# Transformer block on one core: placing feed-forward operands so that the moving operand less the weights is 224 bytes modulo 256

## The chip, the cores and the metric

The kernel runs on one core of a Trainium2 chip. The metric is the device time of one execution in microseconds. Three runs of the kernel before took 2417.2 us in the median, from 2412.65 to 2418.02.

## What is computed

A conditioned transformer block in float32 over 64 sequences of 128 rows, width 512, 16 heads, feed-forward width 2048. The core of the reference:

```python
emb = jax.nn.silu(_sin_emb(timestep)) @ W_ada + b_ada
scale, shift = jnp.split(emb[:, None, :], 2, axis=-1)
x = _ln(src) * (1.0 + scale) + shift
q, k, v = heads of (x @ Wq + bq), (x @ Wk + bk), (x @ Wv + bv)
scores = q k^T / sqrt(HEAD_DIM) + attention_bias, -inf where src_mask
ctx = softmax(scores) @ v
x = x + (ctx @ Wo + bo)
h = _ln(x) * g2 + beta2
ff = _gelu2(h @ W1 + b1) @ W2 + b2          # _gelu2(z) = z * sigmoid(1.702 z)
return x + ff
```

## The kernel before, in words

Five engines run hand-ordered streams of instructions with semaphores between them. No scheduler decides an order. The program has a setup, an attention stage that handles one sequence per half step and writes its result to DRAM, and a feed-forward part in two stages: **up** (h @ W1 and the gate, its results stored to DRAM as `gated`) and **down** (the gate's results @ W2, added to the residual). Both feed-forward stages go over 16 groups of four sequences, with eight units in a group.

Every float32 product is made of three float32r matmuls, high by high, high by low and low by high, of operands that were split beforehand into a high and a low part. In the feed-forward part a 2 x 2 block product is written with seven factor products in place of eight (the Strassen-Winograd scheme). So a unit in either stage has 7 products x 2 halves x 3 = 42 matmuls, each with 128 rows, 128 weight columns and 256 moving columns. `three` issues them and `product` (up) and `down` call it:

```python
1597  def three(out_ap, stat, moving, start, stop):
1598      (sh, sl), (mh, ml) = stat, moving
1599      pe.matmul(out_ap, sh, mh, start=start, stop=False)
1600      pe.matmul(out_ap, sh, ml, start=False, stop=False)
1601      return pe.matmul(out_ap, sl, mh, start=False, stop=stop)
...
1606          last = three(psU[i][:, 0:H], [wc[:, weights.AT[j], h, a, e * P:(e + 1) * P] for h in range(2)],
1607                       [T[u][:, h, b, e, :] for h in range(2)], e == 0, e == 1)
...
          last = three(acc[i][:, half * H:(half + 1) * H], [gs[j % 2][:, h, a, half * P:(half + 1) * P] for h in range(2)],
                       [wc[:, weights.AT[j], h, b, :] for h in range(2)], j == 0 and half == 0, j == J - 1 and half == 1)
```

Going up the factors of the weight matrix, `wc`, are the matmul's weights (the stationary operand), and the factors of the rows, `T0` or `T1` by group, are the moving operand. Coming down, the factors of the gate's results, `gs0` or `gs1` by unit, are the weights, and `wc` is the moving operand. The core loads the weights of the next matmul while the present one streams.

Each of these tensors lies at one address in every partition. All slices that a matmul takes of them begin at a multiple of 256 bytes from the tensor's start (512 bytes for 128 float32 columns, 1024 for 256). So for a given product the difference of the two addresses modulo 256, here called the **residue**, is the same for all its matmuls, for a matmul's own weights and for those of the next.

In the up stage a group of transposes (L246) of the next group's rows stands ahead of two of the eight units, eight transposes each time. Around the matmuls, VectorE and ScalarE empty the accumulators into `gu` and apply the gate, GpSimd adds up parts of `gu`, and SyncE stores a `gu` slot per unit. In the down stage SyncE loads `gated` three units ahead into `gbuf` and slots of `gu`, GpSimd forms two sums, ScalarE rounds to the high part and VectorE takes the low part into `gs` (L1556).

Addresses come from `layer`: tensors are given out one behind another, and `at_once` gives out several and takes them back at once, so that the next call begins at the same place (tensors of different stages share memory). A tensor named `ahead_...`, `over_...`, `end_...` or `zone` is never read or written; it only holds a place.

Of the kernel before, what the change touches and what calls it, by code (L numbers as in the profile page):

```python
# [20 lines left out]
F32 = mybir.dt.float32  # L21
F32R = mybir.dt.float32r
# [5 lines left out]
P = 128  # L28
# [142 lines left out]
def slots(t):  # L171

    return t[:, 0:4, :], t[:, 4:8, :]
# [1485 lines left out]
def layer(nc, d, out):  # L1659

    B, S, DM = d["x"].shape
    CH, H = DM // P, d["bias"].shape[1]
    assert S == P and DM == 4 * P and H == 16 and B % 4 == 0
    resid = nc.dram_tensor("resid", [B, S, DM], F32, kind="Internal").ap()
    ada_rows = nc.dram_tensor("ada_rows", [B, 2 * DM], F32, kind="Internal").ap()
    gated = nc.dram_tensor("gated", [B // 4, 8, P, 10 * P], F32, kind="Internal").ap()
    with ExitStack() as hold, nc.Block() as block, ExitStack() as whole:
        shared = lambda name, shape, dt=F32: whole.enter_context(nc.sbuf_tensor(name, shape, dt))
        ident = shared("ident", [P, P])

        def at_once(*tensors):

            with ExitStack() as used:
                return [used.enter_context(nc.sbuf_tensor(name, shape, dt)) for name, shape, dt in tensors]

        eight = lambda name: (name, [P, 8, 2 * P], F32)
        T1, = at_once(("T1", [P, 2, 7, 2, 2 * P], F32R))
        raw_b, raw_c, raw_d = at_once(*(eight(f"raw1_{n}") for n in "bcd"))
        _, raw_a = at_once(("over_raws", [P, 24, 2 * P], F32), ("raw1_a", [P, 4, 2 * P], F32))
        _, _, r0 = at_once(eight("over_wo_hi"), eight("over_wo_lo"), ("r0", [P, 4, DM], F32))  # L1680
        gs1, gbuf1, u2d, u3d, e5 = at_once(("gs1", [P, 2, 7, 2 * P], F32R), eight("gbuf1"),
                                           *((f"part_{n}", [P, 2, 2 * P], F32) for n in ("u2", "u3", "p5")))
        wo = [shared(f"wo_{part}", [P, CH, DM], F32R) for part in ("hi", "lo")]
        raw_o = shared("raw_o", [P, CH, DM])
        shared("end_T1", [P, 1024])

        turn = [whole.enter_context(nc.psum_tensor(f"turn{i}", [P, CH, P], F32)) for i in range(2)]

        w = at_once(*((f"w{n}_{part}", [P, CH, DM], F32R) for n in "qkv" for part in ("hi", "lo")))
        w = [w[0:2], w[2:4], w[4:6], wo]  # L1690
        r, T0, hTf, b2_bc, p1c, p5c = at_once(("r", [P, 4, DM], F32), ("T0", [P, 2, 7, 2, 2 * P], F32R), eight("hTf"),
                                              ("b2_bc", [P, DM], F32), ("p1c", [P, 2 * P], F32), ("p5c", [P, 2 * P], F32))
        raw2_0, raw2_1, gs0, gbuf0, c1, e2, e4 = at_once(
            eight("raw2_0"), eight("raw2_1"), ("gs0", [P, 2, 7, 2 * P], F32R), eight("gbuf0"),
            *((f"part_{n}", [P, 2, 2 * P], F32) for n in ("c1", "p2", "p4")))
        _, gbuf_x = at_once(("over_gbuf0", [P, 9728], F32), eight("gbuf_x"))
        rd = at_once(*((f"rd{i}", [P, 4, DM], F32) for i in range(2)))
        shared("zone", [P, 12288])
        second = SecondNorm(nc, whole, hold, resid, ident, turn, 4, d["W1"].shape[1], r0, r, hTf, [T0, T1])
        _, wc, gu, s1p = at_once(("ahead_wc", [P, 8], F32), ("wc", [P, 8, 2, 7, 2 * P], F32R), ("gu", [P, 4, 4, 2 * P], F32), ("s1p", [P, 2, 2 * P], F32))  # L1700
        halves = gu[:, :, :, :].rearrange("p (s t) q n -> p s (t q) n", s=2)
        places = (gu, s1p, (p1c, p5c), rd, [gs0, gs1], [gbuf0, halves[:, 1, :, :], halves[:, 0, :, :], gbuf1], gbuf_x,
                  [t[:, :, :] for t in (c1, e2, e4, u2d, u3d, e5)], b2_bc)
        with ExitStack() as ctx:
            sb = lambda name, shape, dt=F32: ctx.enter_context(nc.sbuf_tensor(name, shape, dt))
            bq_s, bk_c, bv_bc = sb("bq_s", [P, CH]), sb("bk_c", [P, CH]), sb("bv_bc", [P, DM])

            wo_in = hold.enter_context(nc.semaphore("wo_in"))
            psD = [ctx.enter_context(nc.psum_tensor("psD0", [P, DM], F32)), turn[1][:, :, :].rearrange("p c k -> p (c k)")]
            first = FirstNorm(nc, ctx, hold, d["x"], ident, turn[0])  # L1710
            xin, adab = (t.rearrange("p (s n) -> p s n", s=8) for t in (
                first.xin[:, :, :, :].rearrange("p u b n -> p (u b n)"), first.adab[:, :, :].rearrange("p b n -> p (b n)")))
            second.turned_early = [xin, adab]
            raws = [(raw_a[:, :, :], first.xn[:, :, :].rearrange("p b (s n) -> p (b s) n", n=2 * P))]
            raws += [slots(t) for t in (raw_d, xin, adab, raw_b, raw_c, raw2_0, raw2_1)]
            weights = Weights(nc, hold, d, raws, wc, 8)
            setup_part(nc, block, hold, d, w, first, ada_rows, bq_s, bk_c, bv_bc, raw_o, wo_in)
            attention_part(nc, block, hold, d, w, first, ada_rows, resid, psD, bq_s, bk_c, bv_bc, raw_o, wo_in, second, weights)

        feed_part(nc, block, hold, d, second, weights, places, resid, gated, turn, out)  # L1720
# [25 lines left out]
```

## Time and profile before

| | before |
|---|---|
| median of 3 runs | 2417.2 us |
| the profiled execution | 2417.7 us |
| its span | 2415.9 us |
| TensorE busy | 2330.2 us (96%), 21,034 matmuls |
| VectorE busy | 1709.8 us (71%) |
| ScalarE busy | 1326.4 us (55%) |
| GpSimd busy | 1880.0 us (78%) |
| mean granted TensorE clock | 0.99 |

The attention stage ends at about 1070 us, the up stage at about 1778 us, and the down stage takes the rest. A matmul's duration in the profile runs from its start to the modelled end of its results, and matmuls overlap; the pace of TensorE is the step from one start to the next, which the timeline's start times give.

### The profile page before, as it was taken

Reading aid. Unit: us, or ns where it says so; the run is one execution under the profiler, and the core shown is the slowest. Engines: PE = TensorE matmul, PEld = TensorE weight load, DVE = VectorE, ACT = ScalarE, POOL = GpSimd, SP = SyncE. Lnnn points to the kernel's source line nnn. Section 1 sums busy time; section 2 is a strip of 40 time slices with the busy share of each in tenths; the row PEclk is TensorE's granted clock in tenths of the full one; section 3 lists DMA queues with packets and bytes.
Section 4 is the critical chain, followed back from the end, with each engine's and each line's share of the span. In section 5 each row is a group of like instructions: output and inputs, shape, how many; then the busy total and the mean of one; then the engine's idle time right before and its main releaser. Section 6 shows DMA issues by size and latency. Waiting matters only on the chain.

```text
span 2415.9 us, 61264 instructions
## 1 busy us (share of the span) xinstructions
PE 2330.2 (96%) x21034; PEld 2193.0 (91%) x21034; DVE 1709.8 (71%) x2864; ACT 1326.4 (55%) x3663; POOL 1880.0 (78%) x1787
## 2 busy tenths in 40 slices
PE   5999999999999999987999999999989999999998
PEld 3888888888888888877999999999979999999998
DVE  5777777777777777767667676767566776666676
ACT  2666666666666666675555555555544443433443
POOL 3777777777777777779777877777898878888886
PEclk9999999999999999998999999999999999999999
DMA  7344444444444444423343434344365656556564
GB/s 239 112 138 142 142 127 126 135 142 142 129 130 138 142 133 126 122 89 124 137 163 148 154 148 159 142 159 154 138 226 174 204 176 202 189 189 205 188 197 131
DMA packets 289442, 372.13 MB, mean 154 GB/s; under 512 B 29072, under 2 KB 203280, under 8 KB 289232
## 3 DMA queue, kind: packets, MB, share of 16 engines
q1 hardware_dynamic: 289232, 369.44, 46.6%
q8 instruction: 118, 1.93, 0.3%
q14 instruction: 92, 0.75, 0.1%
HBM read 251.68 MB, written 117.70 MB: 153 GB/s over the span
## 4 chain that ended last, share of the span: by engine, by line
PE 89%; POOL 3%; DVE 3%; issue 2%; ACT 1%; DMA 1%; SPq 0%; DVEq 0%; POOLq 0%; ACTq 0%
PE up L1600 13%; PE up L1599 13%; PE up L1601 13%; PE psD L956 5%; PE turn L956 5%; PE turn L958 5%; PE turn L957 5%; PE psD L958 5%; PE psD L957 5%; PE psS L985 4%; PE psS L971 3%; PE psC L995 3%; PE turn L1599 2%; PE turn L1600 2%; PE turn L1601 2%
## 5 line engine op out<-in xcount | busy, mean ns | idle before, releaser
L1599 PE MATMUL up<-T,wc 128*128 128x256 f32 x1792 | 507.5, 283 | 14.5 <-DVE gu L1473 7.7
L1600 PE MATMUL up<-T,wc 128*128 128x256 f32 x1792 | 503.6, 281 | 0.0
L1601 PE MATMUL up<-T,wc 128*128 128x256 f32 x1792 | 502.8, 281 | 0.0
L628 POOL TENSOR_TENSOR s<-s,rinv 128x512 f32<-128x512 f32 x254 | 265.1, 1044 | 229.0 <-DVE rinv L823 228.8
L744 ACT ACTIVATE s<-s,nmx 128x128 f32<-128x128 f32 x1024 | 397.4, 395 | 7.3 <-issue 4.3
L1599 PE MATMUL up<-wc,gs 128*128 128x256 f32 x1280 | 354.5, 277 | 2.4 <-DVE gs L1556 2.4
L1599 PEld LDWEIGHTS up<-T,wc 128*128 128x128 f32 x1792 | 339.0, 189 | 18.3 <-DVE gu L1473 8.9
L1600 PE MATMUL up<-wc,gs 128*128 128x256 f32 x1280 | 354.2, 277 | 0.0
L1601 PE MATMUL up<-wc,gs 128*128 128x256 f32 x1280 | 354.0, 277 | 0.0
L688 POOL TENSOR_TENSOR bias<-bias,mneg 128x512 f32<-128x512 f32 x256 | 335.3, 1332 | 11.2 <-DVE mneg L828 11.2
L1600 PEld LDWEIGHTS up<-T,wc 128*128 128x128 f32 x1792 | 339.2, 189 | 0.0
L1601 PEld LDWEIGHTS up<-T,wc 128*128 128x128 f32 x1792 | 338.3, 189 | 0.0
L1556 DVE TENSOR_TENSOR gs<-gbuf,gs 128x768 fp32r<-128x768 f32 (+1 forms) x128 | 177.0, 1407 | 110.8 <-ACT gs L1432 110.8
L1556 DVE TENSOR_TENSOR gs<-gu,gs 128x768 fp32r<-128x768 f32 x126 | 187.7, 1517 | 79.7 <-ACT gs L1432 79.7
L1599 PEld LDWEIGHTS up<-wc,gs 128*128 128x128 f32 x1280 | 241.3, 189 | 2.8 <-DVE gs L1556 2.8
L1600 PEld LDWEIGHTS up<-wc,gs 128*128 128x128 f32 x1280 | 241.3, 189 | 0.0
L1601 PEld LDWEIGHTS up<-wc,gs 128*128 128x128 f32 x1280 | 241.2, 188 | 0.0
L1432 ACT ACTIVATE gs<-gbuf 128x768 fp32r<-128x768 f32 (+1 forms) x128 | 115.5, 948 | 185.2 <-PE up L1601 175.4
L1432 ACT ACTIVATE gs<-gu 128x768 fp32r<-128x768 f32 x126 | 113.9, 950 | 173.1 <-PE up L1601 163.2
L744 ACT ACTIVATION_READ_ACCUMULATOR s<-s,nmx 128x1 f32 x1024 | 199.3, 195 | 0.0
L1279 POOL TENSOR_TENSOR gu<-gu,p5c 128x256 f32<-128x256 f32 x128 | 102.6, 801 | 119.7 <-ACT p5c L1373 82.1
L812 DVE TENSOR_TENSOR s<-psS,bias 128x512 f32<-128x512 f32 x256 | 168.3, 678 | 22.0 <-PE psS L971 20.8
(221 smaller groups left out, 7016.5 us busy)
## 6 DMA issues: line engine op xcount, KB each, us to landing
bias<-in_bias SPq DMA_DIRECT2D x128, 512.0 KB, 5.3
gated<-gu SPq DMA_DIRECT2D x128, 512.0 KB, 2.6
adab<-ada_rows SPq DMA_DIRECT2D x64, 512.0 KB, 5.4
gbuf<-gated SPq DMA_DIRECT2D x64, 512.0 KB, 4.0
gu<-gated SPq DMA_DIRECT2D x63, 512.0 KB, 3.8
xin<-in_x SPq DMA_DIRECT2D x32, 512.0 KB, 5.0
resid<-rout SPq DMA_DIRECT2D x64, 256.0 KB, 2.0
r<-resid SPq DMA_DIRECT2D x16, 1024.0 KB, 6.1
```

Source lines behind the costliest of these rows:

```text
L628: eng.tensor_tensor(s[:, b, heads, :], s[:, b, heads, :], rinv[:, b, heads].unsqueeze(2).to_broadcast([P, HG, S]), ALU.mult).then_inc(done, 1)
L688: pool.tensor_tensor(bias[:, b, heads, :], bias[:, b, heads, :], mneg[:, b, :].unsqueeze(1).to_broadcast([P, HG, S]), ALU.add).then_inc(bi ...
L744: last = act.activation(s[:, b, h, :], s[:, b, h, :], ACT.Exp, bias=nmx[:, b, h:h + 1], accum_out=sums[:, b, h:h + 1])
L812: dve.tensor_tensor(s[:, b, heads, :], psS[g][:, :, :], bias[:, b, heads, :], ALU.add).then_inc(score_ready, 1)
L956: pe.matmul(out, sh, mh, start=start, stop=False)
L957: pe.matmul(out, sh, ml, start=False, stop=False)
L958: return pe.matmul(out, sl, mh, start=False, stop=stop)
L1432: act.activation(gs[s % 2][:, 0, ops, :], t[:, ops.start + 1:ops.stop + 1, :], ACT.Copy).then_inc(s_hi, 1)
L1556: dve.tensor_tensor(gs[s % 2][:, 1, ops, :], t[:, ops.start + 1:ops.stop + 1, :], gs[s % 2][:, 0, ops, :].bitcast(F32), ALU.subtract).then ...
L1599: pe.matmul(out_ap, sh, mh, start=start, stop=False)
L1600: pe.matmul(out_ap, sh, ml, start=False, stop=False)
L1601: return pe.matmul(out_ap, sl, mh, start=False, stop=stop)
```

## The change

Two unused tiles of 48 float32 (192 bytes) are put ahead of `T1` and of `T0`, the unused tile ahead of `wc` grows from 8 to 16 float32 (32 to 64 bytes), and the two place holders `end_T1` and `zone` grow by 256 bytes, so that what lies behind them moves too.

```diff
-        T1, = at_once(("T1", [P, 2, 7, 2, 2 * P], F32R))
+        _, T1 = at_once(("ahead_T1", [P, 48], F32), ("T1", [P, 2, 7, 2, 2 * P], F32R))
...
-        shared("end_T1", [P, 1024])
+        shared("end_T1", [P, 1088])
...
-        r, T0, hTf, b2_bc, p1c, p5c = at_once(("r", [P, 4, DM], F32), ("T0", [P, 2, 7, 2, 2 * P], F32R), eight("hTf"),
+        r, _, T0, hTf, b2_bc, p1c, p5c = at_once(("r", [P, 4, DM], F32), ("ahead_T0", [P, 48], F32), ("T0", [P, 2, 7, 2, 2 * P], F32R), eight("hTf"),
...
-        shared("zone", [P, 12288])
+        shared("zone", [P, 12352])
...
-        _, wc, gu, s1p = at_once(("ahead_wc", [P, 8], F32), ("wc", [P, 8, 2, 7, 2 * P], F32R), ("gu", [P, 4, 4, 2 * P], F32), ("s1p", [P, 2, 2 * P], F32))
+        _, wc, gu, s1p = at_once(("ahead_wc", [P, 16], F32), ("wc", [P, 8, 2, 7, 2 * P], F32R), ("gu", [P, 4, 4, 2 * P], F32), ("s1p", [P, 2, 2 * P], F32))
```

The instructions and their order are the same on every engine. The addresses in a partition, and the residues that follow from them:

| tensor | before | after | moved by |
|---|---|---|---|
| T1 | 17024 | 17216 | 192 |
| T0 | 53888 | 54336 | 448 |
| gs1 | 17024 | 17024 | 0 |
| gs0 | 62080 | 62336 | 256 |
| wc | 95296 | 95840 | 544 |
| gu | 209984 | 210528 | 544 |
| wq, wk, wv | 45696, 62080, 78464 | each + 256 | 256 |
| xT0, xT1 (high) | 134464, 142656 | each + 512 | 512 |

| product | moving less weights, modulo 256, before | after |
|---|---|---|
| up: T less wc | 64 | 224 |
| down: wc less gs | 192 | 224 |
| K and Q projection: xT less wk or wq | 192 | 192 |
| V projection: wv less xT (512 columns) | 64 | 64 |
| output projection: wo less cT (512 columns) | 192 | 192 |

## Rows read from the trace of the kernel before

**Rows 1.** The page: busy time of engines, and the chain that ended last

```profile
PE 2330.2 (96%) x21034; PEld 2193.0 (91%) x21034; DVE 1709.8 (71%) x2864; ACT 1326.4 (55%) x3663; POOL 1880.0 (78%) x1787
...
PE 89%; POOL 3%; DVE 3%; issue 2%; ACT 1%; DMA 1%; SPq 0%; DVEq 0%; POOLq 0%; ACTq 0%
```

**Rows 2.** Stretches: us, busy PE (x instructions), PEld, DVE, ACT, POOL, clock, DMA

```profile
1130.00:1745.00 615.00, 610.37 (x5169) 609.42 (x5168) 411.50 (x863) 343.20 (x649) 482.24 (x607) 1.00 0.40 151
...
1860.00:2416.00 556.00, 546.14 (x4819) 545.94 (x4818) 378.27 (x307) 218.92 (x257) 456.24 (x342) 0.99 0.58 186
```

**Rows 3.** Groups by line: TensorE, L1599 (L1600 and L1601 alike)

```profile
L1599 PE MATMUL up<-T,wc 128*128 128x256 f32 x1792 | 507.5, 283 | 14.5 <-DVE gu L1473 7.7 <-ACT p1c L1368 4.4 <-DVE wc L330 1.3
...
L1599 PE MATMUL up<-wc,gs 128*128 128x256 f32 x1280 | 354.5, 277 | 2.4 <-DVE gs L1556 2.4
...
L1599 PE MATMUL turn<-wc,gs 128*128 128x256 f32 x512 | 142.4, 278 | 10.3 <-DVE gs L1556 5.3 <-DVE wc L330 5.0
```

**Rows 4.** Timeline of TensorE (start us, us, what): up, 180 steps apart

```profile
1504.97 0.28 PE L1599 MATMUL up<-T,wc 128*128 128x256 f32 x1
...
1526.17 0.28 PE L1599 MATMUL up<-T,wc 128*128 128x256 f32 x1
```

**Rows 5.** Timeline: down, first and last, 177 steps apart

```profile
2079.91 0.28 PE L1599 MATMUL up<-wc,gs 128*128 128x256 f32 x1
...
2099.97 0.28 PE L1599 MATMUL up<-wc,gs 128*128 128x256 f32 x1
```

**Rows 6.** Timeline: up, last group, 8 steps apart

```profile
1757.30 0.28 PE L1601 MATMUL up<-T,wc 128*128 128x256 f32 x1
...
1758.21 0.28 PE L1600 MATMUL up<-T,wc 128*128 128x256 f32 x1
```

**Rows 7.** Timeline: down, first group, 37 steps apart

```profile
1784.61 0.28 PE L1600 MATMUL turn<-wc,gs 128*128 128x256 f32 x1
...
1788.97 0.28 PE L1601 MATMUL up<-wc,gs 128*128 128x256 f32 x1
```

**Rows 8.** Timeline: K projection, 6 steps and 10 steps apart

```profile
833.39 0.28 PE L958 MATMUL turn<-xT_hi,wk_lo 128*128 128x256 f32 x1
...
834.07 0.28 PE L958 MATMUL turn<-xT_hi,wk_lo 128*128 128x256 f32 x1
...
835.18 0.28 PE L957 MATMUL psD<-xT_lo,wk_hi 128*128 128x256 f32 x1
...
836.36 0.28 PE L958 MATMUL psD<-xT_hi,wk_lo 128*128 128x256 f32 x1
```

**Rows 9.** Timeline: down, behind a wait, clock at 1.2 GHz, 10 steps apart

```profile
1828.96 0.42 PE L1599 MATMUL turn<-wc,gs 128*128 128x256 f32 x1
...
1831.09 0.41 PE L1600 MATMUL up<-wc,gs 128*128 128x256 f32 x1
```

**Rows 10.** Chain in order of time, up stage: eight transposes

```profile
1404.47 0.87 PE turn L246 x8
```

**Rows 11.** DMA issues: KB each, median us to landing

```profile
gated<-gu SPq DMA_DIRECT2D x128, 512.0 KB, 2.6
...
gu<-gated SPq DMA_DIRECT2D x63, 512.0 KB, 3.8
```

**Rows 12.** Columns as in rows 2: middle of up and down

```profile
1260.00:1680.00 420.00, 420.00 (x3579) 420.00 (x3579) 283.25 (x600) 236.80 (x451) 329.10 (x418) 1.00 0.40 153
1920.00:2340.00 420.00, 420.00 (x3708) 420.00 (x3707) 283.99 (x232) 169.67 (x199) 351.53 (x265) 1.00 0.60 193
```

**Rows 13.** Timeline: V projection, 10 steps, and output projection, 9 steps

```profile
363.03 0.39 PE L957 MATMUL turn<-wv_lo,xT_hi 128*128 128x512 f32 x1
...
365.33 0.39 PE L958 MATMUL turn<-wv_hi,xT_lo 128*128 128x512 f32 x1
...
829.63 0.40 PE L958 MATMUL psD<-wo_hi,cT_lo 128*128 128x512 f32 x1
...
831.73 0.39 PE L958 MATMUL psD<-wo_hi,cT_lo 128*128 128x512 f32 x1
```

## The prediction

> **What bounds the kernel now.** I read the page's busy shares and its chain first, then the busy time by stage, then the start times of single matmuls. TensorE is busy 96% of the span and holds 89% of the chain that ended last [rows 1]. By stage [rows 2], the middle of the up stage has TensorE busy 610 of 615 us and the middle of the down stage 546 of 556 us; every other engine has slack there. So in both feed-forward stages the time is a count of matmuls times the step from one start to the next. (The duration column is no such step: a matmul of 0.28 us starts 0.12 us after the last one, since they are pipelined.)
>
> The two products are made of the same instruction, a float32r matmul of 128 rows, 128 weight columns and 256 moving columns, 5,376 times in each stage: three lines of 1,792 going up, three of 1,280 plus 512 coming down [rows 3]. Their steps differ. Going up, 180 steps of one unbroken stretch take 1526.17 − 1504.97 = 21.20 us, **117.8 ns** each [rows 4]. Coming down, 177 steps take 2099.97 − 2079.91 = 20.06 us, **113.3 ns** each [rows 5]. A slower and a quicker step, 4.45 ns apart: that difference, times the count, is what this change can move.
>
> Is the excess bound to the residue? The residue (moving address less weight address, modulo 256) is 64 going up and 192 coming down. But both steps occur at both. Going up, one short stretch after a wait runs at 0.91 us for 8 steps, 114 ns [rows 6]. Coming down, one stretch runs at 4.36 us for 37 steps, 117.8 ns [rows 7]. The projections of K and Q, also 256 columns and with residue 192, show 10 steps in 1.18 us and, 2 us earlier, 6 steps in 0.68 us [rows 8]. So the residue does not fix the step by itself. The stream of weights for the next matmul and the moving stream of the present one settle into one of two patterns, a stretch keeps the pattern it has fallen into, and the residue at most tilts which. At the clock's lower level the down product takes 2.13 us for 10 steps, 213 ns [rows 9], which is 256 columns at 1.2 GHz with no excess; at the upper level 256 columns alone are 106.7 ns. The excess belongs to the upper clock level and to two streams that meet there, not to the instruction.
>
> **The change part by part.** It removes no instruction, adds none and changes no order on any engine. Only addresses move: T0, T1, wc and what lies behind them.
>
> *Up product.* Its residue goes from 64 to 224. No row shows a 256-column matmul at 224. The nearest rows are those at 192, 32 bytes away, against 96 bytes round the circle from 64; and 192 in its longest stretch is the 113.3 ns step. I take 113.3 ns. Steps that count: 5,169 matmuls between 1130 and 1745 us [rows 2], less about 15 groups of 16 transposes, leaves some 4,930. At 4.45 ns each that is **−21.9 us**. I count nothing for the first and last group (1070 to 1130, 1745 to 1778 us): there TensorE waits for factors and weights that come at their own pace, and a quicker step only lengthens the wait. The bounds of this term: no gain at one end. At the other the lowest step of any full weight load in the trace, the transposes, 8 in 0.87 us, 109 ns [rows 10]: 4,930 × 8.8 = 43 us.
>
> *Down product.* From 192 to 224. By the same nearness it stays at 113.3 ns: 0. Bounds: 109 ns, 4,819 [rows 2] × 4.3 = −20.7 us; 117.8 ns, 4,819 × 4.45 = +21.4 us.
>
> *Everything else that moves.* The attention's tiles move by 256 or 512 bytes, so the residues of its products keep their values: 0. The tiles gu and s1p move by 544 and now start 32 bytes past a multiple of 64. The store of a gu slot lands in 2.6 us and the load of one in 3.8 us [rows 11], while a load is issued three units ahead, 3 × 42 × 113 ns = 14 us; twice the time would still be hidden, and what would show it failing is DVE's idle time ahead of gs. If the up stage shortens by 3.7%, POOL, busy 329 of 420 us there, and DVE, 283 of 420 [rows 12], still have room; the next thing to be late would be POOL's sums in gu, which only lie on the chain in the last group today.
>
> Sum: 2417.7 us (the profiled execution: a span of 2415.9 and 1.8 around it) − 21.9 = 2395.8; that execution lies 0.5 us over the median of 2417.2. Forecast **2396 us**.
>
> **Rivals.**
>
> *Both products get quicker still.* If 224 lets the two streams miss each other altogether, the step is bounded by the weight load alone, 109 ns [rows 10], in both stages: −43 − 20.7, or 2354 us. For it: the change sets both products to one value, and the two known steps look like one and two equal delays over 109 ns (4.3 and 8.8), so none is a natural third pattern. Against it: not one 256-column step near 109 ns stands in the stretches read, at 64 or 192. (The Trainium skill, "TensorE: Matmul & The Clock Gate", section "Wait — 56ns, not 53.3ns?", gives a start-to-start time of N ÷ 2.4 GHz plus about 2.5 ns, which for 256 columns would be an estimate of 109.2 ns; no 256-column row here shows it.)
>
> *Nothing changes.* The pattern is chosen by how a stretch begins, not by the residue. Each up group begins twice behind eight transposes and then falls into the slow step; the down stage begins its long stretch once, at 1831 us [rows 9], and keeps the quick one to the end. If 224 leaves that as it is, the time is 2417 us. For it: one residue shows both steps [rows 6 to 8]. Against it: 256-column stretches at 64 are almost all slow and the down stage's mostly quick. The 512-column projections speak neither way cleanly: V at residue 64 takes 2.30 us for 10 steps, the output projection at 192 takes 2.10 us for 9 [rows 13], 230 against 233 ns, so there 64 is the better one. (The Trainium skill, "TensorE: Matmul & The Clock Gate", section "Step-by-step: what each phase is for", says that TensorE reads moving operand and weights through two independent ports, so that loading the next weights takes nothing from the running matmul. By that rule addresses cannot matter and this rival holds; the trace disagrees at least in this, that one instruction has two steps.)
>
> *Slower: the down product falls into the slow pattern.* Its 5,000-odd matmuls from 1831 us on are one stretch that starts once and never restarts, so one unlucky start at the new residue prices all of them: + 4,819 × 4.45 = 21.4 us with the up product as it is, 2439 us. It decides at the first few steps after 1831 us. For it: the slow step is stable in this very product [rows 7]; and at 512 columns 192 is the worse residue, so nearness may point the wrong way. Against it: that slow stretch lasted only until the next wait, and the long one, begun at the same residue behind a wait at 1.2 GHz [rows 9], ended quick.
>
> *Worse than any pattern seen,* a third delay of the same size in both products: 22 + 43 us more, 2482 us. Nothing in the trace shows it; only the missing rows at 224 leave it open.
>
> **How the numbers follow.** Up quick and down as now, 2396: 0.36. Both at the pace of the weight load, or one of them, 2354 or a little over: 0.20. Nothing changes, 2417: 0.24. Down slow, 2439: 0.15. Worse: 0.05. I leave out the last two, 0.20, and take the range from the second rival's 2354 less the uncertainty of its counts, 2346, to the unchanged time with its spread and a small loss, 2424. Within 0.2% (4.8 us, about what a measurement of this kernel can tell from no change) lies only the rival of no change: same 0.24. Faster 0.36 + 0.20 = 0.56, slower 0.15 + 0.05 = 0.20. With cases of both signs, the likeliest one's own range is 2391 to 2400.
>
> **What would show it.** Right: in the profile after, 180 steps of an unbroken up stretch take 20.4 us in place of 21.20 and 177 of the down stretch still 20.06; up's mean duration falls from 283 and 281 ns to the 277 of the down rows; all else, the attention stage above all, keeps its times. Wrong: up at 117.8 (no change), down at 117.8 (the loss), either at 109 (the larger gain), or a shorter step with new idle time ahead of it from POOL or DVE, which would mean that the up stage has another bound.

## The result, and the profile after

| | before | after |
|---|---|---|
| median | 2415.59 us (4 runs, 2412.65 to 2418.02) | 2444.22 us (4 runs, 2443.21 to 2445.42) |
| profiled execution, and its span | 2417.7 us, 2415.9 | 2443.21 us, 2441.4 |

The ratio after to before is 1.0109, 95% interval 1.0085 to 1.0134: slower, where 2396 us was forecast, and outside the range of 2346 to 2424. The experiments below add something on the time of before: it has two values, about 2417 and about 2438 us, and the four runs of this table all had the lower one.

The page after, busy time of the engines and the chain, laid out as in [rows 1]. TensorE's busy time grew by 29.0 us, the span by 25.5:

```profile
PE 2359.2 (97%) x21034; PEld 2222.6 (91%) x21034; DVE 1741.1 (71%) x2864; ACT 1324.3 (54%) x3663; POOL 1833.6 (75%) x1787
...
PE 90%; POOL 3%; DVE 3%; issue 1%; DMA 1%; ACT 1%; SPq 0%; DVEq 0%; POOLq 0%; ACTq 0%
```

The stretches after, columns as in [rows 2]. First the setup and attention, where TensorE was busy 1032.07 us before, then the middle of up and of down:

```profile
0.00:1070.00 1070.00, 1032.60 (x9970) 903.59 (x9970) 800.46 (x1553) 679.42 (x2626) 792.65 (x698) 0.99 0.45 138
1130.00:1745.00 615.00, 610.47 (x5157) 609.59 (x5156) 406.08 (x862) 343.27 (x650) 478.18 (x605) 1.00 0.40 151
1860.00:2442.00 582.00, 571.65 (x4831) 571.44 (x4830) 410.40 (x307) 220.13 (x258) 412.74 (x343) 0.99 0.56 178
```

Attention is unchanged. In the same 615 us of up, 12 fewer matmuls are done than before, at the same busy time and granted clock. Down does 4,831 of them in 571.65 us of busy time, where before 4,819 took 546.14: each is dearer. The groups by line, beside [rows 3], say the same: up's mean duration went from 283 to 285 ns, down's from 277 and 278 to 282 and 283.

```profile
L1599 PE MATMUL up<-T,wc 128*128 128x256 f32 x1792 | 511.3, 285 | 14.6 <-DVE gu L1473 8.2 <-ACT p1c L1368 3.9 <-DVE wc L330 1.3
...
L1599 PE MATMUL up<-wc,gs 128*128 128x256 f32 x1280 | 360.4, 282 | 2.3 <-DVE gs L1556 2.3
...
L1599 PE MATMUL turn<-wc,gs 128*128 128x256 f32 x512 | 145.1, 283 | 9.8 <-DVE gs L1556 5.0 <-DVE wc L330 4.8
```

The step itself, as in [rows 4, 5], from the timeline after. Up, 171 steps in 1524.96 − 1504.73 = 20.23 us, 118.3 ns:

```profile
1504.73 0.28 PE L1599 MATMUL up<-T,wc 128*128 128x256 f32 x1
...
1524.96 0.28 PE L1599 MATMUL up<-T,wc 128*128 128x256 f32 x1
```

Down, 168 steps in 19.88 us, 118.3 ns:

```profile
2080.04 0.28 PE L1599 MATMUL up<-wc,gs 128*128 128x256 f32 x1
...
2099.92 0.28 PE L1599 MATMUL up<-wc,gs 128*128 128x256 f32 x1
```

At the new residue both products have one and the same step, and it is neither of the two seen before. Step by step it repeats every eight matmuls, alike in both products: 120, 117, 122, 118, 117, 121, 116, 116 ns, mean 118.3.

Summed over all steps between 105 and 127 ns (the pace of TensorE at its upper clock level; start to start, from the trace):

| | step before | step after | steps | gives | stage (first matmul to next stage or end) |
|---|---|---|---|---|---|
| up | 117.75 ns | 118.31 ns | 5,209 | +2.9 us | 689.5 to 693.3 us, +3.8 |
| down | 113.39 ns | 118.33 ns | 5,332 | +26.3 us | 637.4 to 662.6 us, +25.2 |

The two stages grew by 29.0 us, and up began 3.4 us earlier: that makes 25.6 us, where the spans differ by 25.5. Nearly all of the loss is the down product's step.

### The profile page after: what moved, and what is told of

Its sections match the earlier page's. It is cut to its first block, busy times and chain, and to the rows that moved or that the text cites. A ratio compares the mean times of both kernels' runs of the same rounds, so it can differ in the third digit from the quotient of the medians.

```text
span 2441.4 us, 61264 instructions
## 1 busy us (share of the span) xinstructions
PE 2359.2 (97%) x21034; PEld 2222.6 (91%) x21034; DVE 1741.1 (71%) x2864; ACT 1324.3 (54%) x3663; POOL 1833.6 (75%) x1787
## 4 chain that ended last, share of the span: by engine, by line
PE 90%; POOL 3%; DVE 3%; issue 1%; DMA 1%; ACT 1%; SPq 0%; DVEq 0%; POOLq 0%; ACTq 0%
PE up L1599 14%; PE up L1600 14%; PE up L1601 14%; PE psD L956 5%; PE turn L956 5%; PE psD L958 5%; PE psD L957 5%; PE turn L958 5%; PE turn L957 5%; PE psS L985 4%; PE psS L971 3%; PE psC L995 3%; PE turn L1599 2%; PE turn L1601 2%; PE turn L1600 2%; PE turn L136 2%
## 5 line engine op out<-in xcount | busy, mean ns | idle before, releaser
L1599 PE MATMUL up<-T,wc 128*128 128x256 f32 x1792 | 511.3, 285 | 14.6 <-DVE gu L1473 8.2
L1600 PE MATMUL up<-T,wc 128*128 128x256 f32 x1792 | 506.6, 283 | 0.0
L1601 PE MATMUL up<-T,wc 128*128 128x256 f32 x1792 | 506.2, 283 | 0.0
L1599 PE MATMUL up<-wc,gs 128*128 128x256 f32 x1280 | 360.4, 282 | 2.3 <-DVE gs L1556 2.3
L1600 PE MATMUL up<-wc,gs 128*128 128x256 f32 x1280 | 360.1, 281 | 0.0
L1601 PE MATMUL up<-wc,gs 128*128 128x256 f32 x1280 | 360.0, 281 | 0.0
L1599 PEld LDWEIGHTS up<-T,wc 128*128 128x128 f32 x1792 | 340.9, 190 | 17.9 <-DVE gu L1473 9.4
L1600 PEld LDWEIGHTS up<-T,wc 128*128 128x128 f32 x1792 | 341.1, 190 | 0.0
L1601 PEld LDWEIGHTS up<-T,wc 128*128 128x128 f32 x1792 | 341.0, 190 | 0.0
L1556 DVE TENSOR_TENSOR gs<-gbuf,gs 128x768 fp32r<-128x768 f32 (+1 forms) x128 | 198.7, 1578 | 98.1 <-ACT gs L1432 98.1
L1556 DVE TENSOR_TENSOR gs<-gu,gs 128x768 fp32r<-128x768 f32 x126 | 199.3, 1615 | 83.9 <-ACT gs L1432 83.9
L1599 PEld LDWEIGHTS up<-wc,gs 128*128 128x128 f32 x1280 | 241.9, 189 | 2.7 <-DVE gs L1556 2.7
L1600 PEld LDWEIGHTS up<-wc,gs 128*128 128x128 f32 x1280 | 241.8, 189 | 0.0
L1601 PEld LDWEIGHTS up<-wc,gs 128*128 128x128 f32 x1280 | 241.7, 189 | 0.0
L1432 ACT ACTIVATE gs<-gbuf 128x768 fp32r<-128x768 f32 (+1 forms) x128 | 115.3, 946 | 197.7 <-PE up L1601 188.2
```

The lines of the kernel that those rows point to most:

```text
L1432: act.activation(gs[s % 2][:, 0, ops, :], t[:, ops.start + 1:ops.stop + 1, :], ACT.Copy).then_inc(s_hi, 1)
L1556: dve.tensor_tensor(gs[s % 2][:, 1, ops, :], t[:, ops.start + 1:ops.stop + 1, :], gs[s % 2][:, 0, ops, :].bitcast(F32), ALU.subtract).then ...
```

## The experiments

The question was what sets the step. A stretch, below, is a run of matmuls of one product without a wait in it; a long one has 40 steps or more. **Theory** (A in the expectations): the residue, whose values have steps of their own. **Rivals:** the pattern is chosen by how a stretch begins and the residue only tilts it; the product or the absolute addresses decide; or something else that the change moved (gu, s1p) costs the time. All kernels but the last differ from before only in unused places, with the place holders behind them grown as in the change (`end_T1` 1088, `zone` 12352); the pad of T0 is always that of T1, so only T1's line is shown. "Step" is the mean defined above, up / down. A kernel without a number of runs ran once.

**1. The up half as forecast: 192 in both** (T up by 128 bytes).

```diff
-        T1, = at_once(("T1", [P, 2, 7, 2, 2 * P], F32R))
+        _, T1 = at_once(("ahead_T1", [P, 32], F32), ("T1", [P, 2, 7, 2, 2 * P], F32R))
```

> Residue 192 in both products, nothing else changed. If the residue alone sets the step (theory A): up and down both step at 113.3 ns, time 2417 - 5,220 x 4.4 ns = about 2394 us. If the product, by the way its stretches begin, sets the step at 64 and 192 (rival B): up stays at 117.8, down at 113.3, about 2417 us. If any common residue for both products hurts (rival C, the change's loss comes from T and gs or wc sharing a bank in some other way): slower than 2430 us.

2411.86 us, before beside it 2410.6. Step 116.18 / 113.49. Up is a mixture at this residue: of its long stretches, 15 run at 113.3 to 113.9 and 22 at 117.8 ns. In the timeline of this kernel, 171 steps of a slow one in 20.14 us, then 159 of a quick one in 18.02 us:

```profile
1499.79 0.28 PE L1599 MATMUL up<-T,wc 128*128 128x256 f32 x1
...
1519.93 0.28 PE L1599 MATMUL up<-T,wc 128*128 128x256 f32 x1
...
1539.93 0.28 PE L1599 MATMUL up<-T,wc 128*128 128x256 f32 x1
...
1557.95 0.28 PE L1599 MATMUL up<-T,wc 128*128 128x256 f32 x1
```

So 192 gives the up product the quick step, but not always.

**2. The residues exchanged: 192 going up, 64 coming down** (wc up by 128 bytes).

```diff
-        _, wc, gu, s1p = at_once(("ahead_wc", [P, 8], F32), ("wc", [P, 8, 2, 7, 2 * P], F32R), ("gu", [P, 4, 4, 2 * P], F32), ("s1p", [P, 2, 2 * P], F32))
+        _, wc, gu, s1p = at_once(("ahead_wc", [P, 40], F32), ("wc", [P, 8, 2, 7, 2 * P], F32R), ("gu", [P, 4, 4, 2 * P], F32), ("s1p", [P, 2, 2 * P], F32))
```

> The residues of the kernel before exchanged: 192 going up, 64 coming down. Theory A: the steps exchange too, up 113.3 and down 117.8 ns, time within 3 us of the kernel before. Rival B: up keeps 117.8 and down 113.3 ns, the same time. The profile's steps tell them apart, not the time.

2436.38 us, before beside it 2410.6. Step 117.33 / 117.78. The down product at 64 has taken over the up product's step, 171 steps in 20.14 us:

```profile
2079.78 0.28 PE L1599 MATMUL up<-wc,gs 128*128 128x256 f32 x1
...
2099.92 0.28 PE L1599 MATMUL up<-wc,gs 128*128 128x256 f32 x1
```

That rules out the product as the cause of before's two steps: 64 is 117.8 ns in either. Up at 192 is again a mixture, here mostly slow. The time missed the forecast, which had the two steps merely exchanged.

**3 to 5. Other residues alike in both products.** 128 and 0 by wc alone (its pad 56 or 24 float32 in place of 8), 160 by T1's pad of 16 and wc's pad taken away:

```diff
+        _, wc, gu, s1p = at_once(("ahead_wc", [P, 56], F32), ("wc", [P, 8, 2, 7, 2 * P], F32R), ("gu", [P, 4, 4, 2 * P], F32), ("s1p", [P, 2, 2 * P], F32))
...
+        _, wc, gu, s1p = at_once(("ahead_wc", [P, 24], F32), ("wc", [P, 8, 2, 7, 2 * P], F32R), ("gu", [P, 4, 4, 2 * P], F32), ("s1p", [P, 2, 2 * P], F32))
...
+        _, T1 = at_once(("ahead_T1", [P, 16], F32), ("T1", [P, 2, 7, 2, 2 * P], F32R))
+        wc, gu, s1p = at_once(("wc", [P, 8, 2, 7, 2 * P], F32R), ("gu", [P, 4, 4, 2 * P], F32), ("s1p", [P, 2, 2 * P], F32))
```

128 bytes:

> Residue 128 in both. Theory A: both products have one and the same step, at a value not yet known between 109 and 122 ns, so between 2350 and 2462 us. Rival B: the products differ, down quicker.

2450.37 us, step 119.51 / 118.68: not one step for both, as the theory had it. Up holds two steps at this residue too. In its middle groups they alternate, 250 steps in 30.00 us (120.0 ns), then 82 in 9.73 us (118.7 ns):

```profile
1457.99 0.29 PE L1600 MATMUL up<-T,wc 128*128 128x256 f32 x1
...
1487.99 0.28 PE L1601 MATMUL up<-T,wc 128*128 128x256 f32 x1
...
1489.11 0.28 PE L1600 MATMUL up<-T,wc 128*128 128x256 f32 x1
...
1498.84 0.28 PE L1601 MATMUL up<-T,wc 128*128 128x256 f32 x1
```

Behind the transposes the first step is 200 ns in the former and 205 ns in the latter.

0 bytes:

> Residue 0 in both. Theory A: one step for both products, not known; the streams start in the same place, and if that makes them meet at once and stay together it is the worst, 122 ns or more (2460 us); if they part at once, the best, 109 ns (2350 us). Rival B: the products differ, down quicker.

2461.58 us, step 119.89 / 119.98. Nearly every step is 120 ns; coming down, 168 of them in 20.16 us:

```profile
2079.78 0.28 PE L1599 MATMUL up<-wc,gs 128*128 128x256 f32 x1
...
2099.94 0.28 PE L1599 MATMUL up<-wc,gs 128*128 128x256 f32 x1
```

160 bytes:

> Residue 160 in both, 32 bytes on the other side of 192. Theory A (residue decides which patterns a stretch can hold): one behaviour for both products. If 192 lies in the middle of a good region, 160 shows 113.3 ns at least in part, up and down, about 2395 to 2420 us; if 192 is a lone good value between 224 (118.3) and 160, about 118 ns in both and 2440 us. Rival D (down is quicker by its role, with wc as the moving operand): down quicker than up by over 2 ns.

2433.1 us, step 117.86 / 117.39 (before beside it 2437.45 in its one run, the first sign that before has two times).

**6. 32 going up, 96 coming down** (T1's pad 32, wc's 48 float32).

```diff
+        _, T1 = at_once(("ahead_T1", [P, 32], F32), ("T1", [P, 2, 7, 2, 2 * P], F32R))
...
+        _, wc, gu, s1p = at_once(("ahead_wc", [P, 48], F32), ("wc", [P, 8, 2, 7, 2 * P], F32R), ("gu", [P, 4, 4, 2 * P], F32), ("s1p", [P, 2, 2 * P], F32))
```

> The last two untried multiples of 32, one in each product: 32 going up and 96 coming down. Theory A: each gets a step of its own, between 113 and 122 ns; 32, beside 0 (119.9), near 119 to 120, and 96, beside 64 (117.8), near 118, together about 2445 us. Rival D: down is quicker by its role.

2446.24 us, step 117.39 / 119.99. Both were expected near their neighbours, 32 at 119 to 120 and 96 near 118, and both came out 2 ns on the other side. At 96 the steps repeat every six (125, 116, 124, 118, 121, 116 ns), with the same mean as at 0, 168 steps in 20.16 us:

```profile
2079.79 0.28 PE L1601 MATMUL up<-wc,gs 128*128 128x256 f32 x1
...
2099.95 0.28 PE L1601 MATMUL up<-wc,gs 128*128 128x256 f32 x1
```

**7, 8. Beside 192: 176 and 208** (wc a further 16 bytes into a larger tile; T1's pad 24 or 40 float32).

```diff
+        _, T1 = at_once(("ahead_T1", [P, 24], F32), ("T1", [P, 2, 7, 2, 2 * P], F32R))
...
+        wc, gu, s1p = at_once(("wc", [P, 8 * 2 * 7 * 2 * P + 8], F32R), ("gu", [P, 4, 4, 2 * P], F32), ("s1p", [P, 2, 2 * P], F32))
+        wc = wc[:, 4:4 + 8 * 2 * 7 * 2 * P].rearrange("p (j h a n) -> p j h a n", j=8, h=2, a=7)
```

176 bytes:

> Residue 176 in both: 16 bytes under 192, which needs wc to begin 16 bytes into its tensor. Theory A with a grain of 32 bytes: as 160 or as 192, nothing in between. With a finer grain: a step of its own, and if it is the quick one for all stretches, up and down at 113.3 ns or less and 2392 us or less.

2452.47 us, step 118.81 / 119.26.

208 bytes (wc's pad of 8 kept):

> Residue 208 in both, 16 bytes over 192. Theory A with a grain of 32 bytes: as 192 (113.3 and 117.8 mixed) or as 224 (118.3). With a finer grain: a step of its own; between 192 and 224 I expect 113.3 to 118.3 ns, 2395 to 2440 us.

2449.67 us, step 118.11 / 119.16. Sixteen bytes to either side of 192 the quick step is gone.

All residues tried, mean step in ns:

```
residue   0      32     64     96     128    160    176    192            208    224
up      119.9  117.4  117.8   -     119.5  117.9  118.8  113.3 or 117.8  118.1  118.3
down    120.0    -    117.8  120.0  118.7  117.4  119.3  113.3 or 117.8  119.2  118.3
```

192 is a lone good value among the ten tried, not the bottom of a valley. No residue reached below 113 for its mean. Several of the other means going up are mixtures as well: long stretches run at 116.7 or 117.8 ns at 32, 118.7 or 120.0 at 128, 117.3 or 118.7 at 160, 117.8 or 118.3 at 208. At 64 and 224 every long stretch has one step, in either product. At 176 and 208 the two products differ by 0.5 and 1 ns at the same residue; what sets that is not shown.

**9. 192 in both, timed** (the kernel of experiment 1).

> The first experiment again, timed in rounds beside the kernel before, whose own time was 2437 in one run and 2411 to 2418 in all others. Theory A2 (at residue 192 a stretch holds either pattern and its start decides; the down stage is one stretch of 5,060): the times of the kernel before fall into two groups some 22 us apart (5,060 x 4.4 ns), about 2415 and 2437; those of this kernel scatter over up to 45 us, since its up stretches choose too, the lowest near 2395, and its profile shows stretches at 113.3 and at 117.8 ns in up. Rival (the one run of 2437 was disturbed from outside): all runs of the kernel before within 8 us.

Median of 12 runs 2410.28 us (2403.99 to 2431.39, two above 2425); ratio 0.9947, 0.9911 to 0.9984. None came near the 2395 that was hoped for; in the profiled one 17 long stretches going up are quick and 18 slow. The 17 runs of before beside it fall in two groups: eight at 2411.0 to 2418.1 and nine at 2433.1 to 2440.1. A single long down stretch that begins in the other pattern is worth 5,060 × 4.4 ns = 22 us, the distance of the groups.

**10 to 12. 192 in both, and everything moved** (T, wc, gs0 and gs1 all 32, 64 or 96 bytes further; here 64).

```diff
+        _, T1 = at_once(("ahead_T1", [P, 48], F32), ("T1", [P, 2, 7, 2, 2 * P], F32R))
...
+        _, gs1, gbuf1, u2d, u3d, e5 = at_once(("ahead_gs1", [P, 16], F32), ("gs1", [P, 2, 7, 2 * P], F32R), eight("gbuf1"),
...
+            eight("raw2_0"), eight("raw2_1"), ("ahead_gs0", [P, 16], F32), ("gs0", [P, 2, 7, 2 * P], F32R), eight("gbuf0"),
...
+        _, wc, gu, s1p = at_once(("ahead_wc", [P, 24], F32), ("wc", [P, 8, 2, 7, 2 * P], F32R), ("gu", [P, 4, 4, 2 * P], F32), ("s1p", [P, 2, 2 * P], F32))
```

By 32 bytes:

> Residues 192 and 192 as before, but rows, weights' factors and gate's factors all lie 32 bytes further on, against the first experiment. If only the difference of the two addresses matters (theory A): no steps other than 113.3 and 117.8 ns in either product. If an absolute address matters (rival F): steps of another size. How many stretches take which pattern may change, as the starts meet the transposes' operands in another place: time 2394 to 2440 us.

2412.56 us, step 116.90 / 113.47.

By 64 bytes:

> As the run with 32 bytes, with 64: only 113.3 and 117.8 ns by theory A, other steps by rival F; the share of quick stretches in up may differ, 2394 to 2440 us.

2403.88 us, step 113.49 / 113.39: of 46 long stretches going up 45 are quick, and the last, of 40 steps, has a mean of 115.3 ns.

By 96 bytes:

> As the run with 32 bytes, with 96: only 113.3 and 117.8 ns by theory A, other steps by rival F; 2394 to 2440 us.

2427.0 us, step 116.42 / 117.69. Here the one long stretch coming down, 5,059 steps, began slow and stayed so, 168 steps in 19.79 us:

```profile
2079.94 0.28 PE L1599 MATMUL turn<-wc,gs 128*128 128x256 f32 x1
...
2099.73 0.28 PE L1599 MATMUL turn<-wc,gs 128*128 128x256 f32 x1
```

In all three the long stretches have only the two steps 113.3 and 117.8 (but for the mixed one), so it is the difference of the addresses that sets which patterns there are, not the addresses. The difference counts modulo 256 and not modulo 512: in the change itself T0 and T1 differ by 256 bytes modulo 512 as seen from wc, and the groups on either step at 118.3 ns. Which of the two a stretch takes is not set by the residue.

The kernel moved by 32 settles a rival besides. Its wc, gu and s1p lie exactly where the change puts them, and only T and gs lie elsewhere: coming down it steps at 113.47 ns. So it is not the new place of gu, s1p or wc that costs the change its time.

**13. By 64 bytes again, timed.**

> The run at residue 192 in both with everything moved by 64, again, in rounds. Theory S (at 192 the start chooses, and where the operands lie against the transposes' decides the start): up holds 113.4 ns in nearly all stretches in every run, so its times lie within 10 us of 2404, apart from runs in which the one long down stretch starts slow (+22 us, 2426). Rival G (each start is a toss whatever the addresses): times spread between 2400 and 2440 as in the first such kernel, and the profile shows up stretches at 117.8.

Median of 12 runs 2409.49 us (2403.44 to 2436.12); ratio 0.996, 0.9926 to 0.9993. The same kernel as in 11 now shows 29 quick and 10 slow stretches going up (step 114.90 / 113.37). So the nearly clean sweep of 11 was not a property of the addresses. In 13 the nine slow stretches behind transposes all begin with a step of 200 or 201 ns and one of 117 or 118. The quick ones of both kernels begin in several ways: 201 or 202 and then 120 to 122; 201 or 202, then 116 or 117, and 122 or 123 two steps on; or 206 or 207. A slow and a quick one can be alike to the nanosecond for three steps (201, 117, 118) and part at the fourth (118 and 122). What sets the choice stays open.

The long stretch coming down starts in another way. At its beginning the granted clock is 0.50, its lower level of 1.2 GHz, with steps of 213 ns, and it rises within the stretch (columns as in [rows 2]). In the kernel of 12:

```profile
1812.50:1819.20 6.70, 4.71 (x22) 4.72 (x23) 5.61 (x5) 2.48 (x4) 5.55 (x5) 0.50 0.43 116
1819.40:1860.00 40.60, 40.60 (x347) 40.60 (x346) 26.98 (x21) 15.37 (x18) 29.48 (x24) 1.00 0.56 178
...
1818.92 0.41 PE L1601 MATMUL up<-wc,gs 128*128 128x256 f32 x1
1819.13 0.33 PE L1599 MATMUL up<-wc,gs 128*128 128x256 f32 x1
1819.30 0.28 PE L1600 MATMUL up<-wc,gs 128*128 128x256 f32 x1
```

One step, here 168 ns, holds the rise, and the slow pattern stands from the next step on. In the nine other traces with 192 coming down that step took 131 to 205 ns (200 in before), and within five steps the quick pattern stood. Where in a matmul the rise falls differs from execution to execution; that this makes one kernel's two times fits, but with one slow case in ten it is not shown.

**14. Before, with everything moved by 64** (64 and 192 kept; T1's pad 16 float32, the rest as in 11).

```diff
+        _, T1 = at_once(("ahead_T1", [P, 16], F32), ("T1", [P, 2, 7, 2, 2 * P], F32R))
```

> The kernel before with its own residues, 64 up and 192 down, and everything moved by 64. Theory S: up at 117.8 ns as before; down at 113.3 or 117.8 ns by its one long start, which the move may tilt: times at 2415 and 2437 or at one of them alone. Rival F (absolute address): other steps.

Median of 12 runs 2418.71 us, two of them at 2438.1 and 2439.4; ratio 0.9997, 0.9966 to 1.0029. Step 117.75 / 113.35: before's own steps, and its two times as well.

**15. The change's up half alone: 224 going up, 192 coming down** (T1's pad 40 float32, wc as before).

```diff
+        _, T1 = at_once(("ahead_T1", [P, 40], F32), ("T1", [P, 2, 7, 2, 2 * P], F32R))
```

> The change in its up half alone: 224 up, 192 down. Theory A: up at 118.3 ns (+3 us), down at 113.3 or 117.8 ns: 2418 or 2440 us. Rival (the change's loss lies in up, or in what moved along): 2444 us with down at 113.3 ns.

2419.69 us, before's median in the same session 2419.42. Step 118.33 / 113.42. By groups of this kernel, the up line is dear and the down line back at 277 ns:

```profile
L1599 PE MATMUL up<-T,wc 128*128 128x256 f32 x1792 | 509.9, 285 | 15.3 <-DVE gu L1473 6.9 <-ACT p1c L1368 4.2 <-DVE wc L330 1.8
...
L1599 PE MATMUL up<-wc,gs 128*128 128x256 f32 x1280 | 354.1, 277 | 3.6 <-DVE gs L1556 3.6
```

So the down half of the change is the loss, and moving T0, T1 and the attention's tensors behind them costs nothing of its own.

**16. A wait that the quicker up stage uncovered.** In the kernel of 11 the step wins 4.26 ns × 5,203 = 22.2 us going up, and the run only 13.8 (2403.88 against 2417.7). Some 7.5 us come back as breaks between matmuls (over 240 ns, start to start): in the first 110 us of the stage 22.2 us of them against 18.4 before, in the middle 2.4 against 0.7, in the last part 8.6 against 6.6. The same kernel in 13, with a quarter of its long stretches slow, took no longer in its profiled run (2403.44): it has 28.1 us of such breaks in all, 11 has 33.2 and before 25.7. One in the middle, in the timeline of the kernel of 11: VectorE is at the small operations of the row statistics (`spread`) when it should empty an accumulator (L1468), ScalarE copies behind it, and TensorE waits 0.69 us:

```profile
1231.12 0.71 DVE L60 SCALAR_TENSOR_TENSOR part<-part 128x4 f32<-128x4 f32 x1
...
1231.96 0.42 DVE L1468 TENSOR_TENSOR gu<-up,p1c 128x256 f32<-128x256 f32 x1
...
1232.48 0.38 ACT L1368 ACTIVATE p1c<-up 128x256 f32<-128x256 f32 x1 [2.35 <-DVE gu L1468]
1232.92 0.38 PE L1599 MATMUL up<-T,wc 128*128 128x256 f32 x1 [0.69 <-ACT p1c L1368]
```

The last experiment puts `spread` behind that operation, on the kernel of 11:

```diff
-                    if j == (7 if first else 6):
+                    if first and j == 7:
                         norm.spread(dve, n + 2)
...
                 c11(k, j % 4)
+                if not first and has(n, 2) and j == 6:
+                    norm.spread(dve, n + 2)
```

> As the run at 192 with everything moved by 64, and VectorE's variance chain of the group after next stands behind the sum c11 of the seventh unit instead of ahead of it. The trace of that run shows TensorE waiting some 0.7 us once a group there, for ScalarE's copy p1c, that for c11, that behind the chain. Theory W (that wait is what the quick step runs into): the wait goes, 13 groups x 0.8 us, about 2394 us. Rival: the chain delays the next unit's c21 and c12 as much, no change, 2404 us.

Median of 12 runs 2408.09 us, eleven of them 2404.9 to 2409.7 and one 2427.8; ratio 0.994, 0.9908 to 0.9971. Step 113.75 / 113.44. The waits of TensorE in the middle of up (columns: us in total, times, longest), where the kernel of 11 has

```profile
PE up L1599 <- ACT p1c L1368: 1.4, 2, 0.7
```

became two others, 12 and 10 times, in the kernel of this experiment (its L1601 is L1599 of the others):

```profile
PE turn L246 <- DVE r L226: 2.9, 12, 0.3
...
PE up L1601 <- ACT p1c L1368: 2.0, 10, 0.3
```

Start to start that is 23 breaks of 11.0 us in place of 3 of 2.4. The edit as such failed. Against 13 it is 1.4 us in the medians, within the spread of either. It is the fastest median measured, 11 us under before in its session; 13, without the edit, is 10 us under it, so nearly all of that gain is the residue's, 192 in both products.

## Why the prediction was wrong

**The reading of the bound** held. Both stages are a count of matmuls times a step, and what the step did explains the time to within a microsecond or two (+2.9 and +26.3 of steps, +3.8 and +25.2 of stages).

**The step that failed** is "The nearest rows are those at 192, 32 bytes away" and with it "I take 113.3 ns", and for the down product "By the same nearness it stays at 113.3 ns: 0". Neighbouring residues share no step: 176 and 208 are at 118 to 119 ns, 16 bytes from 192. The up term, −21.9 us, measured +2.9; the down term, 0, measured +26.3. Beneath it lay the claim that the streams "settle into one of two patterns" and "the residue at most tilts which". At 192 that is so, and at 64 a short quick stretch behind a wait stands beside the lasting slow one [rows 6]. But the residue does more than tilt: it sets which patterns there are. At 224 there is one, a cycle of eight steps, and the quick one of 113.3 ns lasted at 192 alone of the ten tried. [Rows 6 to 8] were read as one law for all addresses, when they showed only two of them.

**The rivals.** "Slower: the down product falls into the slow pattern", given 0.15, had the place and nearly the size: 2439 us against 2444. Its mechanism was another: not one unlucky start at 117.8 ns, but 118.3 ns all along the stage, with four times within 2.2 us of one another, and 0.56 ns on the up product besides. The hint named for it, that at 512 columns 192 is the worse residue [rows 13], led to the right doubt about nearness by luck: at 256 columns 192 is the best residue tried. The rival was left out of the range for its chance, and that is what put the time outside. "Both products get quicker still" fell: nothing tried came under 113 ns. "Nothing changes" fell for 224, but its mechanism is real at 192: there stretches of one product and one residue hold either pattern, and nearly each keeps the one that it began with (experiments 1, 9 to 13). "Worse than any pattern seen" was too far: the dearest residue tried gave 120.0 ns and 2461.6 us.

**What was costed at nothing** was nothing. Attention kept its busy time (1032.07 and 1032.60 us); the gu slots, moved by 544 bytes, store and load within 0.2 us of [rows 11], and TensorE's idle time ahead of gs stays where it was, 2.3 us at L1599 against 2.4 [rows 3]:

```profile
gated<-gu SPq DMA_DIRECT2D x128, 512.0 KB, 2.6
...
gu<-gated SPq DMA_DIRECT2D x63, 512.0 KB, 4.0
```

**The rule of independent ports.** Moving both operands together (10 to 12, 14) leaves the steps as they are, moving one changes them by up to 6.6 ns: one instruction at the upper clock level steps at 113.3 to 120.0 ns by the difference of two addresses. The Trainium skill, "TensorE: Matmul & The Clock Gate", section "Step-by-step: what each phase is for", says that loading the next weights takes no read bandwidth from the running matmul. To the nanosecond these traces do not agree with it; where the two operands meet, no run here shows.

**The statement on what can be told apart**, 0.2%, does not fit the kernel before. Of all 52 runs of it in this study 16 lie above 2430 us and the others between 2410 and 2422. That the upper time is the long down stretch in the slow pattern is argued from its size (22 us) and from experiment 12, where that stretch was caught; the upper time of before itself was never profiled. Nor is its share steady: 9 of 17 runs in one session, 6 of 29 in another. Against that upper time the change costs only some 6 us (2444.2 against about 2438); against the lower one some 27.

## What to carry to other kernels

Where TensorE bounds a stage, read the step from start to start: its duration column moved by 2 to 5 ns of 280, while the step tells 113 from 118 and, matmul by matmul, shows which pattern runs. An address effect seen at two values says nothing of a third, however near; try the value itself, one product at a time, before pricing it. And where a long stretch can hold one of two steps, a handful of runs can all fall on one side: time such a kernel in a dozen runs, and look at the groups before the median.

## What the runs showed that was not expected

The step of a 128x128x256 float32r matmul at 2.4 GHz depends on the address of its moving operand less that of the weights, at a grain of 16 bytes or finer: 113.3 ns at best, 120.0 at 0 and 96, where half of the 213 ns at 1.2 GHz is 106.7. While the granted clock was at 1.2 GHz the step was 213 ns in the median in all 18 traces, at every residue tried and in both products: the excess belongs to the upper level. At several residues, 192 above all, two patterns are stable. Which one stands is settled within the first few steps, at 192 coming down for the next 5,060 matmuls, worth 22 us.
